# The preparation of the first attention's inputs, merged into the attention pair by pair

## The reference

```python
x = x + _L0_xattn_ref(_layernorm(x, axis=-1), ctx_2048, ctx_2048)
...
qh = q.reshape(b * h, d // h, m)
kh = k.reshape(b * h, d // h, -1)
vh = v.reshape(b * h, c // h, -1)
scale = 1.0 / jnp.sqrt(jnp.asarray(d // h, dtype=q.dtype))
qk = jnp.einsum('bdm,bdn->bmn', qh, kh) * scale
sm = jax.nn.softmax(qk, axis=-1)
ret = jnp.einsum('bmn,bcn->bcm', sm, vh)
```

## Time and profile before

| | us |
|---|---|
| median of 3 runs (1997.76 to 2004.27) | 2002.18 |
| the profiled execution | 2001.07 |
| its span in the trace | 1999.0 |
| preparation, barrier and first loads, up to the first score | 134.9 |
| from the first score to the scores of unit 4 | 30.7 |
| slots 4 to 63 | 376.5 |
| from the last score to the first instruction of the next stage | 35.6 |

### The profile page before, as it was taken

The page is one execution under the profiler, slowest core; times in us unless marked ns, Lnnn a source line. Parts: engine busy times, 40 slices in busy tenths (PEclk is TensorE's granted clock), DMA queues, the critical chain, the costliest instruction groups (busy, mean ns, idle before and its releaser), DMA issues. The chain is left out here.

```text
span 1999.0 us, 33980 instructions
## 1 busy us (share of the span) xinstructions
PE 1352.8 (68%) x11677; PEld 867.7 (43%) x11698; DVE 1357.4 (68%) x2850; ACT 1119.1 (56%) x1552; POOL 494.0 (25%) x903
## 2 busy tenths in 40 slices
PE   4338999999929995888705666459999546774111
PEld 4315555555517773455501333336666423442100
DVE  6646888888624443478767999726666477775896
ACT  4515777777712121677635888724444337775554
POOL 4412233333320004111002443100101011112663
PEclk9999999999959997899955666679999877777555
DMA  5652555555430002333210000011111210000111
GB/s 167 206 128 61 122 132 132 129 131 132 98 92 1 0 1 39 62 76 74 44 66 2 0 1 1 0 56 31 38 44 27 87 31 1 1 1 11 43 53 42
DMA packets 96395, 118.12 MB, mean 59 GB/s; under 512 B 29728, under 2 KB 82152, under 8 KB 91660
## 3 DMA queue, kind: packets, MB, share of 16 engines
q1 hardware_dynamic: 96268, 116.46, 23.3%
HBM read 80.07 MB, written 22.88 MB: 52 GB/s over the span
## 5 line engine op out<-in xcount | busy, mean ns | idle before, releaser
L610 DVE TENSOR_REDUCE ratt_nmax<-ratt_psS 128x2 f32<-128x512 f32 x512 | 318.3, 684 | 97.3 <-PE ratt_psS L502 97.0
L576 ACT ACTIVATE ratt_E<-ratt_psT 128x1024 f32<-128x1024 f32 x256 | 255.0, 1023 | 108.3 <-PE ratt_psT L524 108.2
L502 PE MATMUL ratt_psS<-ratt_K,ratt_Q 72*128 72x256 bf16 x1024 | 204.0, 283 | 41.5 <-DMA ratt_K<-context_parts 35.9
L524 PE MATMUL ratt_psT<-ratt_Q,ratt_K 75*128 75x256 bf16 x1024 | 195.7, 274 | 7.2 <-DMA ratt_Q<-ratt_rows 6.9
L502 PEld LDWEIGHTS ratt_psS<-ratt_K,ratt_Q 72*128 72x128 bf16 x1024 | 79.9, 99 | 137.5 <-issue 66.0
L537 PE MATMUL ratt_psO<-ratt_E,ratt_V 128*32 128x256 f32 x2048 | 137.9, 387 | 0.7 <-ACT ratt_E L576 0.7
L524 PEld LDWEIGHTS ratt_psT<-ratt_Q,ratt_K 75*128 75x128 bf16 x1024 | 99.4, 98 | 25.1 <-DMA ratt_Q<-ratt_rows 7.4
L3405 PE MATMUL final_psT<-final_identh,final_Z 128*128 128x128 f16 x64 | 8.2, 309 | 110.6 <-ACT final_Z L3439 110.6
L537 PEld LDWEIGHTS ratt_psO<-ratt_E,ratt_V 128*32 128x32 f32 x2048 | 53.6, 109 | 50.4 <-issue 27.4
L897 ACT COPY sffn_XS<-sffn_psG 128x512 f32<-128x512 f32 x8 | 4.7, 586 | 125.6 <-PE sffn_psG L846 125.6
L2207 PE MATMUL nffn_psH<-nffn_W,nffn_QT 128*128 128x512 bf16 x121 | 53.2, 586 | 30.6 <-ACT nffn_H L2286 20.0
(11 more groups left out here) (472 smaller groups left out, 3739.7 us busy)
## 6 DMA issues: line engine op xcount, KB each, us to landing
ratt_Q<-z_parts SPq DMA_DIRECT2D x32, 576.0 KB
ratt_K<-context_parts SPq DMA_DIRECT2D x96, 192.0 KB
gatt_V<-in_ctx_dram SPq DMA_DIRECT2D x16, 512.0 KB, 6.7
z_parts<-prep_ZS SPq DMA_DIRECT2D x48, 128.0 KB, 2.6
context_parts<-prep_CS SPq DMA_DIRECT2D x48, 128.0 KB, 2.3
head_sums<-ratt_O SPq DMA_DIRECT2D x64, 72.0 KB
all_X<-in_x_dram SPq DMA_DIRECT2D x8, 512.0 KB
prep_C<-in_ctx_dram SPq DMA_DIRECT2D x8, 512.0 KB
```

Of the source, the lines that this page charges most:

```text
L502: mm = nc.tensor.matmul(psS[:, RING[h], c * D:(c + 1) * D], Q9[0:R, buf, h, k % 2, c * P:(c + 1) * P], K9[0:R, buf, h, k % 2, :], start=Tr ...
L524: mm = nc.tensor.matmul(psT[:, p % 2, e, c, :], K9[0:RM, buf, h, u, c * P:(c + 1) * P], Q9[0:RM, buf, h, u, :], start=True, stop=True)
L576: nc.scalar.activation(E[:, 2 * b + p // 2, 2 * (p % 2):2 * (p % 2) + 2], psT[:, p % 2], ACT.Exp, scale=SCALE).then_inc(exped, 1)
L610: nc.vector.tensor_reduce(nmax[:, k % 2, h, :], psS[:, RING[h]].rearrange("p (c t) -> p c t", c=2), AX.X, ALU.max, negate=True).then_inc(m ...
```

## The change

`prepare` and `row_attention` are replaced by one function, `first_attention`, with one block and no barrier between them. Its lists start at slot -12 (SP's at -15) and are written out without a loop. The preparation is done for one pair (256 rows) at a time, in steps r: step r of pair a stands in slot 4a - 12 + r, behind what the attention has in that slot.

| step | slot mod 4 | engine | what |
|---|---|---|---|
| -3 | 1 | SP | load_x, load_c, ahead of the rest of the slot |
| 1 | 1 | TensorE, ScalarE, VectorE | transpose of C in the middle of the slot, its copy to CT, bn_stats |
| 2 | 2 | ScalarE, GpSimd, VectorE | first_of_c, rest_of_c, bn_aggr |
| 3 | 3 | GpSimd, SP | root (four small operations), second_of_c; store_c |
| 4 | 0 | GpSimd, ScalarE, SP | third_of_c, weigh; normalise; store_c |
| 5 | 1 | ScalarE, SP | first_of_z; store_c |
| 6 | 2 | GpSimd, VectorE, SP | rest_of_z and its cast, sum_context; store_z |
| 7, 8 | 3, 0 | GpSimd, SP | third_of_z; store_z twice |

Q and K of a pair are loaded in slots 4a - 3 to 4a, as before, and its scores are taken in slots 4a to 4a + 3. Normalising moves from VectorE to ScalarE, the rests and second casts of Z to GpSimd, the weighted sum from TensorE to GpSimd (`weigh`) and VectorE (`sum_context`). There is one buffer for the parts of C and one for those of Z: `first_of_c` waits until the three stores of the pair before have landed, and so does `first_of_z`. The transposes of C have no PSUM of their own; they take a turn in the two halves of psT (`job`).

```diff
-
...
+        def at(n, r):
+
+            a, left = divmod(n + LEAD - r, 4)
+            return a if left == 0 and is_pair(a) else None
...
+                def load_x(a):
+                    if a > 1:
+                        sp.wait_ge(x_in[a % 2], a // 2 * 16)
+                    sp.dma_start(X[:, 2 * a:2 * a + 2, :],
+                                 x_dram[2 * a:2 * a + 2].rearrange("t p d -> p t d")).then_inc(x_in[a % 2], 16)
+
+                def load_c(a):
+                    if a > 1:
+                        sp.wait_ge(c_third, a - 1)
+                    sp.dma_start(C[:, a % 2],
+                                 c_dram[2 * a:2 * a + 2].rearrange("t p d -> p t d")).then_inc(c_in[a % 2], 16)
+
+                def store_c(a, part):
+                    sp.wait_ge((c_first, c_second, c_third)[part], a + 1)
+                    sp.dma_start(ck.rearrange("r s a h u m -> s a h r (u m)")[part, a],
+                                 CS[:, part].rearrange("p u m -> p (u m)")).then_inc(c_out, 16)
+
+                def store_z(a, part):
+                    sp.wait_ge((z_first, z_second, z_third)[part], a + 1)
+                    sp.dma_start(zq.rearrange("s r a h u m -> s a h r (u m)")[part, a],
+                                 ZS[:, part].rearrange("p u m -> p (u m)")).then_inc(z_out, 16)
...
+                def load_q(g):
+                    pair, b = g // 2, g % 2
+                    sp.wait_ge(z_out, pair * 48 + 48)
...
+                    pair, b = g // 2, g % 2
+                    sp.wait_ge(c_out, pair * 48 + 48)
...
+                for n in range(-LEAD - 3, UNITS + 11):
+                    if at(n, -3) is not None:
+                        load_x(at(n, -3))
+                        load_c(at(n, -3))
...
+                        if at(n, 3 + part) is not None:
+                            store_c(at(n, 3 + part), part)
+                        if at(n, 6 + part) is not None:
+                            store_z(at(n, 6 + part), part)
...
+                def rest_of_z(a):
+                    pool.wait_ge(z_first, a + 1)
+                    gp.tensor_tensor(Z[:], Z[:], ZS[:, 0], ALU.subtract).then_inc(z_rest, 1)
+                    pool.wait_ge(z_rest, a + 1)
+                    gp.tensor_copy(ZS[:, 1], Z[:]).then_inc(z_second, 1)
...
+                def rest_of_c(a):
+                    pool.wait_ge(c_first, a + 1)
+                    pool.wait_ge(written, job["turn", a] + 1)
+                    gp.tensor_tensor(C[:, a % 2], C[:, a % 2], CS[:, 0], ALU.subtract).then_inc(c_rest, 1)
...
+                    if at(n, 2) is not None:
+                        rest_of_c(at(n, 2))
+                    if at(n, 3) is not None:
+                        root(at(n, 3))
+                        second_of_c(at(n, 3))
+                    if at(n, 4) is not None:
+                        third_of_c(at(n, 4))
+                        weigh(at(n, 4))
+                    if at(n, 6) is not None:
+                        rest_of_z(at(n, 6))
+                    if at(n, 7) is not None:
+                        third_of_z(at(n, 7))
...
+                def turn_context(a):
+                    j = job["turn", a]
+                    pe.wait_ge(c_in[a % 2], a // 2 * 16 + 16)
+                    if j > 1:
+                        pe.wait_ge(exped, j - 1)
+                    for k in range(KC):
+                        for t in range(2):
+                            mm = nc.tensor.transpose(psT[:, j % 2, 0, k, t * P:(t + 1) * P],
+                                                     C[:, a % 2, t, k * P:(k + 1) * P], ident[:])
...
+                def first_of_z(a):
+                    act.wait_ge(z_done, a * 2 + 2)
+                    if a > 0:
+                        act.wait_ge(z_out, a * 48)
+                    sc.copy(ZS[:, 0], Z[:]).then_inc(z_first, 1)
+
+                def first_of_c(a):
+                    act.wait_ge(c_in[a % 2], a // 2 * 16 + 16)
+                    if a > 0:
+                        act.wait_ge(c_out, a * 48)
+                    sc.copy(CS[:, 0], C[:, a % 2]).then_inc(c_first, 1)
...
+                        if p == 1 and at(n, 1) is not None:
+                            take_context(at(n, 1))
...
+                    if at(n, 2) is not None:
+                        first_of_c(at(n, 2))
+                    if at(n, 4) is not None:
+                        normalise(at(n, 4))
+                    if at(n, 5) is not None:
+                        first_of_z(at(n, 5))
...
+                    if at(n, 1) is not None:
+                        take_stats(at(n, 1))
+                    if at(n, 2) is not None:
+                        aggregate(at(n, 2))
+                    if at(n, 6) is not None:
+                        sum_context(at(n, 6))
...
-        prepare(nc, io, X, CT, ident, zq, ck, ST, wsum)
-        row_attention(nc, io, X, CT, ident, identb, zq, ck, o_dram, r_dram)
+        first_attention(nc, io, X, CT, ident, identb, zq, ck, o_dram, r_dram, ST, wsum)
```

More of the change, by code:

```diff
@@ L427, in _ @@
[L427 to L434 removed]
+                        to = o_dram.rearrange("a (w g) c m -> a g c w m", g=4)[a, g]
@@ L562, in _ @@
-                slots(pe, slot, UNITS + LAG + 1)
+                            turn_max(n - 1)
             @block.scalar
             def _(act):
-                def row(u, b, half):
-                    act.wait_ge(turned, u + 1)
-                    if past(u, 2):
-                        act.wait_ge(row_in[b], half * 32)
-                    nc.scalar.copy(rows[:, b, :], psM[0:6 * NH0]).then_inc(row_out, 1)
-                def exp(m, b, p):
-                    act.wait_ge(shifted, m * 4 + (p + 1))
-                    if p == 0 and past(m, 2):
-                        act.wait_ge(pv, m - 1)
-                    nc.scalar.activation(E[:, 2 * b + p // 2, 2 * (p % 2):2 * (p % 2) + 2], psT[:, p % 2], ACT.Exp,
-                                         scale=SCALE).then_inc(exped, 1)
@@ new lines, in exp, with take_context @@
+                def exp(m, p):
+                    j = job["shift", m, p]
+                    act.wait_ge(written, j + 1)
+                    if p == 0 and m > 1:
+                        act.wait_ge(pv, m - 1)
+                    sc.activation(E[:, m % 2 * 2 + p // 2, 2 * (p % 2):2 * (p % 2) + 2], psT[:, j % 2], ACT.Exp,
+                                  scale=SCALE).then_inc(exped, 1)
+                def take_context(a):
+                    j = job["turn", a]
+                    act.wait_ge(written, j + 1)
+                    sc.copy(CT[:, :, a * 2 * P:(a + 1) * 2 * P], psT[:, j % 2, 0]).then_inc(exped, 1)
@@ new lines, in leave, with normalise @@
+                def leave(m):
+                    a, w = m // 4, m % 4
+                    act.wait_ge(pv, m + 1)
+                    if w == 0 and a > 1:
+                        act.wait_ge(to_dram[a % 2], a // 2 * 64)
+                    O_ = O[:, a % 2].rearrange("p (b q) u m -> p b q u m", b=2)
+                    sc.copy(O_[:, w // 2, :, w % 2, :], psO[:]).then_inc(o_out, 1)
+                def normalise(a):
+                    act.wait_ge(z_shift, a + 1)
+                    if a > 0:
+                        act.wait_ge(z_third, a)
+                    for t in range(2):
+                        sc.activation(Z[:, t], X[:, 2 * a + t, :], ACT.Identity, bias=shift[:, 1, t:t + 1],
+                                      scale=rstd[:, t:t + 1]).then_inc(z_done, 1)
@@ L589, in slot @@
+                sc.activation(keep[:, 0:1], decay[:], ACT.Exp, scale=-1.0).then_inc(expd, 1)
+                for n in range(-LEAD, UNITS + LAG + 1):
                     m = n - LAG
@@ L613, in slot @@
[L613 to L622 removed]
+                            maximum(n, h)
```

635 lines of the change are left out of this document (268 added, 367 removed).

## The result

| | median us | ratio to before, 95% interval |
|---|---|---|
| before | 1998.76 | |
| the changed kernel | 2004.15 (1994.88 to 2013.0) | 1.0024, 1.0013 to 1.0035 |

The change makes the kernel 0.13 to 0.35% slower, a difference at the edge of what can be told. The forecast was 1958, its range 1912 to 1988; both were wrong. The profiled execution has a span of 2003.9 us.

The account below looks back on a forecast made before the run. Preparation leaves room in all engines, while TensorE is full in the steady slots. Span 1999.0 - 103 (lead) + 60 (4.25 a pair x 12 = 51, and 9 for the clock) = 1956; forecast 1958 us, range 1912 to 1988.

Parts of the forecast that it names:

- What it removes: Preparation as its own stage: first score at 36 us, unit 4 at 62.5 in place of 165.6, -103 us.
- Rival C: The lead stays long, its DMAs queued: first score at 60 us, not 36; 1980 us in all, chance 0.1.
- Point 1: Four transposes per pair in slot 1 mod 4, on a full TensorE: 0.85 us a pair.
- Point 2: First_of_z on ScalarE waits 2.3 us for landed stores; TensorE stands 0.9 us a pair at the shift.
- Point 3: Three GpSimd operations ahead of the split in slot 2 mod 4; TensorE waits 2.5 us a pair at turn_max.
- Point 4: Statistics, cast, normalise, root and third_of_z fit idle gaps of VectorE, ScalarE and GpSimd: 0 to 0.3 us a pair.
- Point 5: Extra DMA load in the steady slots, engines 0.69 busy, K issued two slots ahead: nothing (0 to 1).
- Point 6: TensorE loses its higher clock after a third of 12 waits, 2.3 us a slot: 9 us in all.
- The count: Pairs prepared in steady slots that pay the added cost: 12, at 4.25 us each, 51 us before the clock.
- B: Rival: the clock falls at every pair, 12 x (4.25 + 2.3) = 79 us; 1977 us in all, chance 0.2.
- D: Rival: Z's stores land after 9.7 us, ScalarE stands 7.1 us more a pair; 2043 us, slower, chance 0.05.
- A: Rival: waits for stores and split are hidden, only transposes count, 10 us; 1908 us in all, chance 0.15.

Follow-up runs that it names:

- the fastest version: A wait for each part, C's rest a slot later and K's loads a slot sooner, against the changed kernel: 1899.8 us; 1899.2 with the return of sums also later.
- both edits: The changed kernel with a count of landed stores for each part of Z and C, and C's rest a slot later on GpSimd: 1954.7 us, 0.9776.
- all three edits: The changed kernel with a wait for each part, C's rest a slot later, and K's loads issued a slot sooner, ahead of Q's: 1899.8 us, 0.949.

## Why the prediction was wrong, by its own steps

- **What it removes**: right. First score 36.2 (36), unit 4 at 62.3 (62.5), 103.3 us (103). Part of that is luck: from the first score to the first shift it took 16.1 us where 18 were put, and from there to unit 4 10.1 where 8.5 were. It also took TensorE to reach its higher clock at unit 4, as before; it reached it 6.5 us later, which cost the 2.7 us in slot 4. Rival C is out.
- **Point 1**, transposes: 0.6 in place of 0.85, near enough.
- **Point 2** had the right mechanism and stopped halfway. For Z's store it put landing at 15.6 us into the slot and ScalarE's wait at 2.3; the mean was 3.0, and TensorE stood 1.45, not 0.9. Its landing time of 2.6 us from the preparation was too low for this queue; Z's last part takes 3.4 in the median. What it left out altogether is the second cast with the same wait. The working counted the queue up to Z's store and no further, and nobody priced that C's last store stands behind Q's load: 2.1 us of ScalarE, 0.75 of TensorE directly, and 0.9 more through GpSimd.
- **Point 3**: 2.5 forecast, 2.5 measured, but not for its reasons, so the agreement is luck. GpSimd's chain alone makes 1.6 of it; the rest is C's wait. And 2.5 is a mean: it is 3.0 in eight of the eleven pairs and 0.5 to 1.7 in three, where the clock had already fallen at the shift and TensorE came later.
- **Point 4**, covered work: right, no wait of it shows. In the fastest version, where all of it is still there, four slots take 25.2 us.
- **Point 5**, DMA at nothing: right for TensorE in the changed kernel (its weight loads waited 2.2 us for K in 11 pairs), wrong as a statement on the design. It made the landings long, and K became the bound as soon as the other waits went: 28.8 us in 11 pairs with both edits.
- **Point 6**, the clock: the largest miss, and with the second cast of point 2 the step that failed. 0.75 a pair forecast, 2.8 measured, 27 us over 13 pairs. The forecast let the clock fall in 4 pairs of 12; it fell in every one of 13. A third of the pairs at 2.3 us was read from three rows of 2.2 to 2.45 us. The kernel has three waits in a pair, not one, and 3.0 us at turn_max is longer than any of those rows; waits of 3.0 us were followed by a slower slot 13 times of 13, at 3.2 us. The Trainium skill (TensorE: Matmul & The Clock Gate, Why this matters for your kernels) warns of long idle gaps between bursts of matmuls. For waits of 3.0 us the runs agree with it. Below that the clock fell too, but not each time: after 1.9 us in 7 of 13, after 1.6 in 5 of 12 and 2 of 12, after 0.8 in none.
- **The count**: 12 pairs, where 13 groups of slots pay.

Of the rivals, B's clock is what happened (a fall in each pair, and 2.8 us a pair where it said 2.3), though not its total, as it kept the other terms. D named stores that land late and set its point at landing after 6.3 us; Z's last store had 3.4 and C's 4.9, and the time still came out beyond 1988, through the second wait and the clock. D's weight of 0.05 was too low for a mechanism that could hit twice in a pair. A is what the design gives when its waits are really hidden: it said 1908, and the version with all three edits runs at 1900.

The sum of misses: 0.55 + 0.75 for waits behind exponentials, 2.05 for the clock, less 0.25 for the transposes and 0.3 of idle time (0.5 that was there before, 0.2 for K now), makes 2.8 a pair and 31 us in the eleven pairs of the stretch. The groups at its two ends cost 11.8 us where the twelfth pair was put at 5.0, 6.8 more, and slot 4 cost 2.7. That makes 40, the 40 between 476.5 and 437 us. The forecast span was 1956 and this execution's is 2003.9; the other 8.5 us lie in the unchanged stages.

## What to carry to other kernels

When work is merged into a full steady loop, follow every issue of the DMA queue through a whole period and price each wait for a landed store, not just the first; waits that share one cause stand in series, and removing one of them may buy nothing (here Z's alone), or uncover a load that was in time only because the loop was slow. Give each part of a buffer its own count of landed stores, and a waiter only the part that it overwrites. Price a wait of a full TensorE with the clock that follows it, from waits of its own length.

## What the runs showed of the hardware that I had not expected

- The time from a store's issue to its landing grew with what was queued ahead of it. Medians for 128 KB: 3.4 us behind four output DMAs of 72 KB, 4.9 behind Q's 576 KB, 6.4 behind K's and Q's 1152 KB; in the preparation of before it was 2.6. No run separates the place in the queue from what else is in flight. The issue itself can be slower: 1.47 us for a store that takes 0.59 elsewhere.
- The clock's price is not linear in the wait: with the same program around it, nothing after 0.8 us, 1.3 us in the mean after 1.9, 3.2 after 3.0. A wait as short as 1.6 us can be followed by the lower clock, in 5 of 12 cases in one version.
